# Attention steps of a two-layer decoder: turned tail rows on a second pair of PSUM banks, a wait on the gate logits moved, and next rows normalised before row maximum 6

## The reference, cut to what matters

```
x = x + L0_attn(layernorm(x))           # self, window |i-j| <= 32
x = x + L0_xattn(layernorm(x), ctx)     # cross, padded keys masked
x = x + L0_ffn(layernorm(x))            # 8 experts, top 2 of a softmax gate
x = x + L1_attn(layernorm(x))           # self, causal
x = x + L1_xattn(layernorm(x), ctx)     # cross, a 256x77 mask
x = x + L1_ffn(layernorm(x))            # gated, quantised weights and activations
```

## Time and profile before

| | us |
|---|---|
| median of 3 runs (2146.65 to 2151.36) | 2151.16 |
| profiled execution, its own time | 2144.96 |
| its span in the trace | 2143.2 |
| PE busy | 1959.4 (91%) |
| DVE busy | 1260.2 (59%) |
| ACT busy | 981.3 (46%) |
| POOL busy | 687.0 (32%) |

### The profile page before, as it was taken

One profiled execution on the slowest core, in us unless ns is written; L12 is line 12 of the kernel. 1 busy time (PEld: TensorE's weight loads), 2 busy tenths in 40 slices (PEclk: granted clock), 3 DMA queues, 4 the chain that ended last, 5 costly groups with the idle time before them and its releaser, 6 DMA issues. The chain is left out here.

```text
span 2143.2 us, 57238 instructions
## 1 busy us (share of the span) xinstructions
PE 1959.4 (91%) x19754; PEld 1608.0 (75%) x19754; DVE 1260.2 (59%) x5456; ACT 981.3 (46%) x1905; POOL 687.0 (32%) x1244
## 2 busy tenths in 40 slices
PE   7999998999967999999999789899989997999889
PEld 5788876777757999999999567777777775444377
DVE  5788885676541111111115588888878886459964
ACT  2555555666522333333333245555656663357400
POOL 3666664255552000000000545453323220013400
PEclk9999999999878999999999999999999999999999
DMA  7333332333318999999997543343333331000023
GB/s 221 106 112 110 110 122 86 100 106 109 112 55 338 399 342 344 340 341 342 341 341 270 155 132 122 124 130 109 105 91 111 112 112 40 0 0 0 0 63 94
DMA packets 209554, 334.73 MB, mean 156 GB/s; under 512 B 59501, under 2 KB 193426, under 8 KB 200306
## 3 DMA queue, kind: packets, MB, share of 16 engines
q1 hardware_dynamic: 194914, 301.82, 40.8%
q0 software_dynamic: 9552, 26.10, 3.9%
q10 hardware_dynamic: 4928, 4.72, 0.6%
HBM read 193.74 MB, written 28.05 MB: 103 GB/s over the span
## 5 line engine op out<-in xcount | busy, mean ns | idle before, releaser
L2344 ACT ACTIVATE moe_h<-moe_h_ps,moe_weights 128x128 f32<-128x128 f32 x424 | 132.5, 363 | 254.6 <-PE moe_h_ps L2312 226.2
L2777 PE MATMUL ffn_prod_ps<-x_sb,ffn_weights 128*128 128x512 f32 x480 | 210.8, 599 | 7.0 <-ACT ffn_sig_q L2763 7.0
L2376 DVE TENSOR_TENSOR moe_y<-moe_y_ps,moe_weights 128x256 f32<-128x256 f32 x53 | 22.5, 424 | 328.2 <-PE moe_y_ps L2324 328.2
L1397 ACT ACTIVATE causal_prob<-causal_ps 128x768 f32<-128x768 f32 (+1 forms) x192 | 168.7, 879 | 71.9 <-PE causal_ps L1720 71.6
L2312 PE MATMUL moe_h_ps<-moe_h,moe_weights 128*128 128x128 f32 x1696 | 198.0, 275 | 0.0
L2255 POOL DMA_DIRECT2D moe_y_dram<-moe_y x71 | 39.4, 555 | 491.7 <-DVE moe_y L2376 483.5
L2312 PEld LDWEIGHTS moe_h_ps<-moe_h,moe_weights 128*128 128x128 f32 x1696 | 193.6, 192 | 0.1
L2777 PEld LDWEIGHTS ffn_prod_ps<-x_sb,ffn_weights 128*128 128x128 f32 x480 | 91.0, 192 | 124.5 <-issue 110.3
L1068 DVE CUSTOM_DVE_ANT_0 causal_masked<-causal_ps,causal_causal_mask 128x256 bf16<-128x256 f32 (+1 forms) x512 | 152.0, 352 | 39.2 <-PE causal_ps L1686 38.9
L1068 DVE CUSTOM_DVE_ANT_0 window_masked<-window_ps,window_window_mask 128x160 bf16<-128x160 f32 x512 | 134.9, 318 | 44.5 <-PE window_ps L1686 43.3
L1686 PE MATMUL causal_ps<-k_pair,q_pair 64*128 64x78 f32 (+2 forms) x1024 | 101.8, 299 | 27.8 <-DVE causal_m_tok L1068 20.6
(11 more groups left out here) (417 smaller groups left out, 4795.9 us busy)
## 6 DMA issues: line engine op xcount, KB each, us to landing
moe_weights<-moe_w_in SPq DMA_DIRECT2D x53, 2180.0 KB, 9.8
q_pair<-parts SPq DMA_DIRECT2D x512, 128.0 KB, 2.1
parts<-moe_w_in SPq DMA_DIRECT2D x17, 2180.0 KB, 9.3
k_pair<-parts SPq DMA_DIRECT2D x256, 128.0 KB, 2.1
k_pair<-parts SPq DMA_DIRECT2D x256, 38.5 KB, 1.9
moe_y_dram<-moe_y POOLq DMA_DIRECT2D x71, 128.0 KB, 4.1
moe_rows<-moe_slots_dram SPq DMA_DIRECT2D x53, 128.0 KB, 3.9
x_before_ffn_dram<-x_sb SPq DMA_DIRECT2D x16, 256.0 KB, 2.1
```

The costliest lines, as they stand in the source:

```text
L1397: nc.scalar.activation(out, src, ACT.Exp).then_inc(expd, 1)
L2344: nc.scalar.activation(out[:, f, :], psum[:, f // 2, (f % 2) * TM:(f % 2) * TM + TM], ACT.Gelu, bias=bias[:, f:f + 1]).then_inc(done, 1)
L2777: op = nc.tensor.matmul(prod_ps[:, slot, f, :].rearrange("p (b t) -> p b t", b=2), w[:, k, at:at + P], x_cols(n // GROUPS, k), start=(k == ...
```

## The change

1. The tail rows are turned into psb in wide steps, psa in narrow ones.
2. In wide steps `last_turn` goes from slot 6 to the start of slot 4, behind scores(4) and ahead of shifted(4). There it waits for q_lo of item t, oT_ev and v_ev (the other users of psb). `keep_turned` goes ahead of exponentials 4. What now writes psb after it (`value` phase 0, `heads_out`) waits for last_ev; `first_quads` no longer does and waits for `added` instead, `heads_out` in wide steps no longer waits for `added`.
3. `last_quads` no longer waits for seen; output phase 0 does.
4. In narrow steps `next_rows` goes from the end of slot 7 to slot 6 ahead of row_max(6).

```diff
         xT_ps = by_64(psa[:, :, 0:S])
-        turn_ps = by_64(psa[:, :, 0:S])
...
+        def turn_ps(ref):
+
+            return by_64((psb if wide(ref) else psa)[:, :, 0:S])
...
                     for i in range(PAIRS_H):
-                        if i == 4 and wide(ref):
+                        if i == (4 if wide(ref) else 6):
                             next_rows(t, ref)
                         if active(ref, 1):
                             row_max(t, ref, i)
...
                         if i >= 4 and in_merge(ref, 2):
                             merge_rows(t + 2, ref + 2, i - 4)
-                        if i == 7 and not wide(ref):
-                            next_rows(t, ref)
...
-                    if in_tail(ref, 5) and not wide(ref):
+                    if in_tail(ref, 5):
                         keep_turned(t, ref)
                     if shift:
                         exponentials(t, ref, 4)
...
                     if active(ref, 1) and wide(ref):
                         max_rows(t, ref, 1, 0)
-                    if in_tail(ref, 5) and wide(ref):
-                        keep_turned(t, ref)
                     if shift:
                         exponentials(t, ref, 6)
...  first_quads
-                    if wide(ref) and in_tail(ref, 5):
-                        pe.wait_ge(last_ev, tail_item(t, 5) + 1)
+                    if wide(ref):
+                        wait(pe, added, upto(t, ref, 4))
...  last_quads
-                    if wide(ref) and (inline(ref, 6) or inline(ref, 7)):
-                        pe.wait_ge(seen, tail_item(t, 6) + 1)
...  last_turn
-                    wait(pe, m_ev, upto(t, ref, 1, 2) - 1 if wide(ref) and active(ref, 1) else upto(t, ref, 2, 2))
-                    wait(pe, added, upto(t, ref, 4))
-                    wait(pe, o_ev, upto(t, ref, 3, 2))
-                    if routing(ref, 6) or routing(ref, 7):
-                        pe.wait_ge(seen, tail_item(t, 6) + 1)
+                    if wide(ref):
+                        wait(pe, q_lo, upto(t, ref, 0))
+                        wait(pe, oT_ev, upto(t, ref, 4))
+                        wait(pe, v_ev, upto(t, ref, 1))
+                    else:
+                        wait(pe, m_ev, upto(t, ref, 2, 2))
+                        wait(pe, added, upto(t, ref, 4))
+                        wait(pe, o_ev, upto(t, ref, 3, 2))
+                        if routing(ref, 6) or routing(ref, 7):
+                            pe.wait_ge(seen, tail_item(t, 6) + 1)
                     gate(pe, pe_passed)
-                    turn_halves(turn_ps, last_xn[ring(ref, 5)]).then_inc(last_mm, 1)
+                    turn_halves(turn_ps(ref), last_xn[ring(ref, 5)]).then_inc(last_mm, 1)
...  value, phase 0
                         pe.wait_ge(q_lo, t + 1)
+                        if wide(ref) and in_tail(ref, 5):
+                            pe.wait_ge(last_ev, tail_item(t, 5) + 1)
...  output, phase 0, wide
                             wait(pe, o_ev, upto(t, ref, 3, 2))
+                            if inline(ref, 6) or inline(ref, 7):
+                                pe.wait_ge(seen, tail_item(t, 6) + 1)
...  heads_out
-                    wait(pe, added, upto(t, ref, 4))
+                    if wide(ref) and in_tail(ref, 5):
+                        pe.wait_ge(last_ev, tail_item(t, 5) + 1)
+                    if not wide(ref):
+                        wait(pe, added, upto(t, ref, 4))
...  wide_slot
                     if i == 4:
+                        if in_tail(ref, 5):
+                            last_turn(t, ref)
                         shifted(t, ref, 4)
...
                             heads_out(t, ref)
-                        if in_tail(ref, 5):
-                            last_turn(t, ref)
                         shifted(t, ref, 6)
```

More of the change, by code:

```diff
@@ L1450, in keep_turned @@
                     out = x_sb[:, bass.ds(e * ST, ST), :] if tail else rowsT
-                    nc.scalar.activation(out.rearrange("p k (s a t) -> p a (k s) t", a=2, t=64), turn_ps, ACT.Copy).then_inc(last_ev, 1)
+                    nc.scalar.activation(out.rearrange("p k (s a t) -> p a (k s) t", a=2, t=64), turn_ps(ref), ACT.Copy).then_inc(last_ev, 1)
                 def keep_xT(t):
```

## The result

The changed kernel takes 2130.62 us (median of 5 runs, 2129.54 to 2138.17) against 2151.16 (2146.29 to 2152.99) on the same chip: ratio 0.9918, interval 0.9895 to 0.9940. Six later runs of the same file (E9) gave 2133.26, ratio 0.9931 (0.9911 to 0.9951). Faster by 0.7 to 0.8%, as forecast, and within 2 us of the 2132. The terms came out less well than the sum.

The account below looks back on a forecast made before the run. PE's queue was taken to set the pace, with stalls waiting for DVE or ACT. Terms -4.2 - 2.9 - 2.5 - 10 - 4.3 + 6.5 - 2 = -19.4 us gave 2131.8 on the median, forecast 2132, range 2117 to 2150.

Parts of the forecast that it names:

- Padded steps: Padded cross steps: PE's waits of 0.50 and 0.52 ahead of last and first quads go, -10 us in ten steps.
- The clock: Padded cross steps: half of PE's falls to half clock stay away, at 1.4 each, -4.3 us, bounds -8.5 and +6.
- Masked steps: Masked cross steps: the turn waits for q_lo, making steps 15.2 instead of 14.7, +6.5 us with ref 21.
- rival C: Clock falls in each of 11 masked rounds and all ten padded steps: slower, 2161 us, chance 0.07.
- Window steps: Window self steps: earlier next rows remove the stall at scores 1, 0.4 to 0.5 a step, -4.2 us in ten.
- Causal steps: Causal self steps: earlier next rows win 0.25 a step, -2.9 us in 11 steps, bounds -8 and +2.
- +1 instead of -2.9: Causal steps if the second normalising instruction waits behind a whole select: no gain, about 0.1 lost each.
- The change of layers: Ref 17, twice: PE's wait for normalised rows goes, -2.5 us for both, bounds -3.5 and 0.
- Rival A: Cross gains shrink: clock falls stay as they are, causal steps win nothing (+1); 2140 us, chance 0.18.
- B: Masked steps: q_lo is no wait, DVE runs ahead, PE keeps 0.5 a round; 2120 us, chance 0.09.
- D: No change: DVE passes its delay on in all self steps, q_lo takes half the padded gain; 2149 us, chance 0.11.

Follow-up runs that it names:

- E9: The changed kernel again, unaltered, for a second profile; 2133.26 us, ratio 0.9931.
- E1: Against the kernel before, only the next rows normalised ahead of row maximum 6 in narrow steps, turns and waits in wide steps as before; 2148.99 us, ratio 0.9984.
- E3: Against the kernel before, only the logits' wait moved from the last quads to output phase 0; 2135.6 us, ratio 0.9938.
- E4: The whole change, but in layer 1's attention (masked steps) the tail rows are turned in slot 6 into psa as before; 2124.66 us, ratio 0.9902.
- E8: E4 with the padded layer's wait for logits and ranks put back ahead of the last quads; 2141.37 us, ratio 0.9957.
- E6: E4, with next rows in causal steps up to ref 13 normalised behind row maximum 7, ahead of the last expert-row merging; 2123.59 us, ratio 0.9874.
- E5: The whole change, but in all wide steps the tail-row transposes come behind shifted 4 instead of ahead of it; 2131.96 us, ratio 0.9912.
- E12: The changed kernel, but in masked steps the tail-row transposes come behind output phase 0 instead of ahead of shifted 4; 2132.11 us, ratio 0.9926.
- E2: The change's turn and moved logits wait without its next-rows move (next rows at the old place); 2137.14 us, ratio 0.9953.
- E7: E4 with 128 semaphore-counting instructions put into PE's program ahead of layer 1, to shift its instruction blocks; 2142.07 us, ratio 0.9969.
- E10: E6 with layer 1's 16 starting warming products of 128 columns made 32 of 64, to move instruction block ends; 2131.05 us, ratio 0.9919.

## Why the prediction was right, and where not

**Padded steps, right.** Undisturbed steps were to take 15.0 and take 15.1 (15.9 in E1). E3 and E4 split it: the logits' wait gives 0.4 a step, the turn another 0.4. Both are a little less than the 0.50 and 0.52 that PE stood; scores 0 now waits 0.3 for DVE.

**The clock, right in mechanism, mis-sized.** I expected half of the falls to stay away, at 1.4 each. There were six in the ten routed steps, all stayed away, and each had cost 1.7: 10.2 us instead of 4.3, more than the term's own bound of 8.5. E3 and E8 show that the 0.5 wait behind the gate's narrow products decides it. The Trainium skill (TensorE: Matmul & The Clock Gate, "What's actually happening") has the half clock as the default and activity as what lifts it; the runs agree: with 0.5 less idle time the falls are gone. Neither a row nor a rule told how near the stretch was.

**Masked steps, right.** Forecast 15.2 from 14.7, measured 15.43. The circle that I worked out, 11.0 plus 0.45 plus 3.97, gives 15.4; the round shown is 11.11 plus 4.46. Of the +0.74 a step, 0.6 is the turn (138.85 against 133.4 without it), close to the 0.55 that I took. The last 0.13 was in no term. It shows in E1, E3, E4 and E6 too, in which the turn is as before, but the wait for the addition has gone from `heads_out` to the first quads; no run put that wait back, and the cause is open. E5 and E12 show that no later place of the turn gives back more than 0.1. The likely reason is that on the second bank pair it must follow the query part, and everything that the addition needs stands behind one or the other. The one fall of the clock in the masked stretch of E2 and of E9 is a trace of rival C; it needed eight.

**Window steps, mis-sized: -1.8 for -4.2.** The mechanism was right, the 0.5 was not a stall. I took it from two start-to-start distances (1.24 against 0.71) of a group that ran into different neighbours. The row itself said 0.17, and the distance to the next group but one says 0.2 to 0.3. The size holds beyond one pair of profiles: this stretch takes 184.7 to 186.0 us in the kernels with the edit and 186.4 to 187.1 in those without.

**Causal steps, mis-sized: -1.2 for -2.9.** The releaser changed as forecast and the wait ahead of scores 7 became 1.03. Nearly all of the delay of row maximum 6 is passed on; 0.12 a step is left of the 0.25. E6's order gives twice the gain.

The rule of the Trainium skill weighed there (SBUF — State Buffer, "SBUF: two separate sides") does show, but it priced nothing new. A normalising instruction takes 0.41 us when no select of POOL runs, or when it starts ahead of one (all but 4 of 1366 cases; in these 4 the select began 0.03 to 0.06 us behind it). When a select is already running and has 0.3 us or more to go, the instruction ends 0.144 to 0.152 after the end of the select, in all 241 such cases of the 14 profiles. So it waits for the select, and in these steps the wait costs 0.31, not a whole select. In the step before (1446.75) it hits the first of the two instructions, in the step after (1417.34) the second, each then takes 0.72, and the pair takes 1.04 and 1.05. What I had read as a slowing of tenths was this wait, the old place had it too, and the "+1 instead of -2.9" counted it as new.

**The change of layers, split.** In layer 0 ref 17 took 4.1 less (23.22 to 19.12) where I had 1.6. That is partly chance: over all profiles it takes 20.1 on average with the earlier rows (eleven, 19.0 to 21.5) and 22.1 without (three, 20.8 to 23.2), 2.0 apart. In layer 1 ref 16 and 17 took 5.0 more, and that was missing from the sum. There PE needs the stacked queries as soon as they are transferred, and one block of some engine's program (16 KB) is loaded by queue 8 just then. The DMA view of the changed kernel, 1520 to 1522 (busy tenths of the 16 DMA engines in 40 slices), and its row of the load in 1518 to 1520 (packets, MB, share of 16 engines):

```profile
DMA  9989995300010010101010101000000016999999
```

```profile
q8 instruction: 1, 0.02, 4.5%
```

4.5% of 16 engines over 2 us is 1.45 us of one engine; in the trace the load runs from 1519.16 to 1520.61. The "1" in every other slice behind it fits one engine that works alone through its part of the transfer while the other 15 are done, but the profile doesn't tell the engines apart. Over all 14 profiles:

| | load between first issue and use | PE waits | issue to use | no such load | PE waits | issue to use |
|---|---|---|---|---|---|---|
| ref 16 | 11 | 1.20 to 2.26 | 4.86 to 5.91 | 3 (before, E1, E3) | 0.36 to 0.41 | 4.04 to 4.06 |
| ref 17 | 8 | 2.50 to 3.72 | 4.72 to 5.50 | 6 (before, E1, E3, E4, E7, E10) | 1.25 to 2.05 | 4.04 to 4.06 |

The two groups nowhere overlap. The time from issue to use says more than PE's wait: without a load it is the same 4.05 us in all nine cases, and a load inside adds 0.7 to 1.9. The rest of the spread in PE's waits is how late the transfer is issued. So of E6's 3.72 and E10's 1.95 at ref 17, 1.4 is the load (5.43 against 4.05 from issue to use) and 0.4 the later issue. E1 and E4 tell what kind of cause it is: their programs for layer 1 hold the same instructions, PE's for layer 0 is 11 instructions longer in E4 (13001 for 12990), and the wait at ref 16 is 0.37 and 1.68. Which engine's program is loaded stays open, and no run moved the load and nothing else. In the changed kernel the clock also fell at the start of ref 17 (at 1522.7, for 3.4 us), in E9 it did not.

**Sum.** -19.4 forecast, -15.4 measured on the profiled executions. In the sum, the window and causal steps fell short by about 4 and the block loads, with what followed them, added 5.0. Against that stand the clock term, 5.9 too small, and about 2.5 more than forecast at layer 0's ref 17. The median came 20.5 lower in the first runs and 16.7 lower in E9. That it landed within 2 us of the forecast is partly luck. Rival A had the clock wrong, and its +1 for the causal steps is no nearer to the -1.2 measured than the -2.9. B is excluded by the masked stretch, C by its clock of 1.00, D by the window and padded steps, though in the causal steps DVE did pass on most of its delay.

## What to carry to other kernels

Size a stall by the bracket of the row or by the distance to the group after the next, not by one start-to-start distance. A short wait inside a stretch of narrow products can cost three times its length through the clock, as here (0.5 against 1.7), so take such waits first. A move that gives 0.4 in one stage costs 0.6 in another with a different tight engine: make a reordering conditional on the stage. Expect an edit of the program to move its block loads, worth 0.7 to 1.9 us here for each transfer that is needed at once, and look for them by the time from issue to use.

## What the runs showed that I had not expected

- A block load of a program is one packet of 0.02 MB that took 0.9 to 1.7 us here, and with it inside, the transfer of the stacked queries ended 0.7 to 1.9 us later. The Trainium skill (Runtime: NRT & Kernel Launch, "Instruction fetch mechanics") gives blocks of 16 KiB and calls their cost mostly hidden. The size agrees; for these two steps the cost is not hidden.
- 128 semaphore increments on PE with nothing to wait for took 19.7 us.
- A normalising instruction of DVE that starts while a select of POOL runs on for 0.3 us or more ends 0.144 to 0.152 us after the select, every time.
- One wait of 0.5 us, put back, makes five falls of 1.7 us in eight steps.
